# First block: context work two ticks earlier, its merge last in the tick, rounding as a one-element maximum, normalisation and epsilon on GpSimd

## What is computed

```python
# block 0
h = _ln(x, ln1_w, ln1_b) * (1 + sc1) + sh1
q, k, v = split(h @ Wqkv + bqkv)                 # 16 heads of 16
x = x + _attn(q, k, v) @ Wos + bos               # phase 0
h = _ln(x, ln2_w, ln2_b) * (1 + sc2) + sh2
x = x + _attn(h @ Wq + bq, context @ Wk + bk, context @ Wv + bv) @ Woc + boc   # phase 1
h = _ln(x, ln3_w, ln3_b) * (1 + sc3) + sh3
x = x + gelu(h @ W1 + b1) @ W2 + b2              # phase 2
# block 1: the same with 16 heads of 64, rotary q and k, a normalised context: phases 3, 4, 5
```

## Time and profile before

| | |
|---|---|
| median of 3 runs | 4402.54 us (4395.08 to 4405.3) |
| profiled execution | 4394.15 us, span of the core 4392.0 us |
| TensorE clock, mean | 0.987 |
| busy in the span | PE 94%, DVE 67%, ACT 63%, POOL 63% |
| POOL, one instruction | L1180 1.05 us, L1185 and L1190 1.3, L1209 1.02, L1220 0.75 |
| DVE, one instruction | L995 1.21 us, L1091 0.41, L1051 0.39, L1007 0.17, L1023 0.27 (two per batch) |
| DMAs of CX, issue to landing | 4.2 us (384 KB) and 3.8 us (128 KB) |
| DMA of X from the scratch | 4.0 us |

### The profile page before, as it was taken

One profiled execution on the slowest core, in us unless ns is written; L12 is line 12 of the kernel. 1 busy time (PEld: TensorE's weight loads), 2 busy tenths in 40 slices (PEclk: granted clock), 3 DMA queues, 4 the chain that ended last, 5 costly groups with the idle time before them and its releaser, 6 DMA issues.

```text
span 4392.0 us, 95934 instructions
## 1 busy us (share of the span) xinstructions
PE 4145.6 (94%) x34934; PEld 3514.9 (80%) x34934; DVE 2959.7 (67%) x6250; ACT 2745.7 (63%) x10788; POOL 2758.7 (63%) x2555
## 2 busy tenths in 40 slices
PE   7999989888889999999999999999999999999999
PEld 5777777777779987888888888778787878787998
DVE  7999988889865556555556565666666666665443
ACT  5999888888863335656565666656565656564332
POOL 4666666666667775555555565666666666665776
PEclk9999999999999999999999999999999999999999
DMA  2110011111111122222222222322222222221110
GB/s 74 33 33 30 31 41 37 45 45 36 44 55 49 40 73 80 73 75 73 73 75 73 73 78 86 101 75 85 74 86 74 86 73 86 74 91 61 49 46 33
DMA packets 229269, 276.65 MB, mean 63 GB/s; under 512 B 37948, under 2 KB 160320, under 8 KB 228800
## 3 DMA queue, kind: packets, MB, share of 16 engines
q1 hardware_dynamic: 228732, 270.51, 18.0%
q10 hardware_dynamic: 68, 0.02, 0.0%
HBM read 85.89 MB, written 50.33 MB: 31 GB/s over the span
## 4 chain that ended last, share of the span: by engine, by line
PE 65%; DVE 20%; ACT 8%; issue 5%; POOL 2%; DMA 0%; ACTq 0%; SPq 0%; POOLq 0%; DVEq 0%
PE BANKS L573 15%; PE BANKS L575 14%; PE BANKS L574 14%; PE BANKS L724 6%; PE BANKS L712 6%; PE BANKS L760 5%; DVE NM L995 4%; DVE PT L1002 3%; ACT PR L880 2%; ACT PR L864 2%; DVE WL L1044 1%; DVE Z L1101 1%; ACT HF L908 1%; DVE ST L1091 1%; PE BANKS L769 1%
## 5 line engine op out<-in xcount | busy, mean ns | idle before, releaser
L1180 POOL TENSOR_TENSOR PR<-PR,RL 128x512 f32<-128x512 f32 x1024 | 1069.5, 1045 | 946.0 <-DVE RL L1007 942.5
L880 ACT ACTIVATE PR<-BANKS,NM 128x128 f32<-128x128 f32 x2048 | 730.0, 384 | 487.8 <-DVE NM L1058 431.0
L864 ACT ACTIVATE PR<-BANKS,NM 128x128 f32<-128x128 f32 x2048 | 728.9, 415 | 3.9 <-DVE NM L995 3.8
L573 PE MATMUL BANKS<-HH,WH 128*128 128x512 f32 x1632 | 691.7, 424 | 38.0 <-DVE SN L1072 26.7
L1058 DVE TENSOR_REDUCE NM<-BANKS 128x8 f32<-128x1024 f32 x256 | 312.7, 1222 | 532.2 <-PE BANKS L724 532.1
L760 PE MATMUL BANKS<-ID,PR 128*128 128x128 f32 x4096 | 632.9, 278 | 40.6 <-DVE OL L1051 22.8
L575 PE MATMUL BANKS<-HH,WL 128*128 128x512 f32 x1632 | 644.5, 395 | 0.0
L574 PE MATMUL BANKS<-HL,WH 128*128 128x512 f32 x1632 | 644.2, 395 | 0.0
L760 PEld LDWEIGHTS BANKS<-ID,PR 128*128 128x128 f32 x4096 | 496.0, 142 | 165.1 <-issue 61.9
L864 ACT ACTIVATION_READ_ACCUMULATOR PR<-BANKS,NM 128x1 f32 x2048 | 520.1, 257 | 0.0
L1203 POOL TENSOR_TENSOR GL<-GF,GH 128x512 fp32r<-128x512 f32 x256 | 342.4, 1338 | 206.1 <-DVE GH L1147 206.1
(11 more groups left out here) (123 smaller groups left out, 10825.9 us busy)
## 6 DMA issues: line engine op xcount, KB each, us to landing
SW<-SN SPq DMA_DIRECT2D x1024, 128.0 KB, 2.0
x_scratch<-X SPq DMA_DIRECT2D x80, 512.0 KB, 3.2
X<-x_scratch SPq DMA_DIRECT2D x80, 512.0 KB, 4.0
CX<-in_ctx SPq DMA_DIRECT2D x32, 384.0 KB, 4.2
X<-in_x SPq DMA_DIRECT2D x16, 512.0 KB, 3.8
out<-X SPq DMA_DIRECT2D x16, 512.0 KB, 2.9
CX<-in_ctx SPq DMA_DIRECT2D x32, 128.0 KB, 3.8
STG<-in_L_xcond_W SPq DMA_DIRECT2D x4, 512.0 KB, 5.0
```

Source lines behind the costliest of these rows:

```text
L573: e.matmul(o, lh, rh, start=first and i == 0, stop=False)
L864: made = e.activation(pr[:, r], bank[:, r], ACT.Exp, bias=nm[:, h:h + 1], accum_out=RL[npr(t)[0]][:, h:h + 1])
L880: made = e.activation(pr[:, r], bank[:, r], ACT.Exp, bias=nm[:, h:h + 1], accum_out=RL[npr(t)[0]][:, h:h + 1])
L1180: e.tensor_tensor(p3, p3, RL[npr(t)[0]][:, :].unsqueeze(2).broadcast_to([128, 4, 128]), ALU.mult).then_inc(s_nrm, 1)
```

## The change

Four things, all in phases 0 and 1 (`p < 2`):

- `load_c`, `c_turn`, `c_hf` and `c_split` of phase 1 are two ticks earlier; `c_merge` keeps its tick, tg-10.
- On DVE `c_merge` moves from before `v_out` to behind `c_split`, for phase 4 too.
- The casts L1110, L1140 and L1012 become `tensor_reduce` with a maximum over an axis of one element; its output is fp32r as before.
- Epsilon (L1115) and the four normalisations per group (L1101) are done by GpSimd; there `norm` stands behind `root` and ahead of `bias`.

```diff
             if p in CROSS:
-                at["load_c", tg - (22 if p == 1 else 16)].append((p, g))
+                at["load_c", tg - (24 if p == 1 else 16)].append((p, g))
...
-                    at["c_turn", tg - (14 if p == 1 else 8) + c].append(Part(p, g, c, 0))
-                    at["c_hf", tg - (13 if p == 1 else 8) + c].append(Part(p, g, c, 0))
-                    at["c_split", tg - (12 if p == 1 else 7) + c].append(Part(p, g, c, 0))
+                    at["c_turn", tg - (16 if p == 1 else 8) + c].append(Part(p, g, c, 0))
+                    at["c_hf", tg - (15 if p == 1 else 8) + c].append(Part(p, g, c, 0))
+                    at["c_split", tg - (14 if p == 1 else 7) + c].append(Part(p, g, c, 0))
                 at["c_merge", tg - (10 if p == 1 else 5)].append((p, g))
...
+            def rounded(o, i, p):
+
+                if p < 2:
+                    return e.tensor_reduce(o, i.unsqueeze(2), AX, ALU.max)
+                return e.tensor_copy(o, i)
...
-                for p, g in at["c_merge", tick]:
-                    u, k = h_of(p, g, True)
-                    q.wait_ge(s_hl, 2 * u + 2)
-                    e.tensor_copy(HH[k][64:128, 1, :], HL[k][64:128, 1, :].bitcast(F)).then_inc(s_hm, 1)
-
                 for x in at["v_out", tick]:
...
                 for x in at["norm", tick]:
+                    if x.p < 2:
+                        continue
...
-                    e.tensor_copy(HH[k][:, x.c, :], HF[u % 2][:, x.c, :]).then_inc(s_hh, 1)
+                    rounded(HH[k][:, x.c, :], HF[u % 2][:, x.c, :], x.p).then_inc(s_hh, 1)
 
                 for p, g in at["root", tick]:
+                    if p < 2:
+                        continue
...
-                    e.tensor_copy(HH[k][:, x.c, :], HF[u % 2][:, x.c, :]).then_inc(s_hh, 1)
+                    rounded(HH[k][:, x.c, :], HF[u % 2][:, x.c, :], x.p).then_inc(s_hh, 1)
+
+                for p, g in at["c_merge", tick]:
+                    u, k = h_of(p, g, True)
+                    q.wait_ge(s_hl, 2 * u + 2)
+                    rounded(HH[k][64:128, 1, :], HL[k][64:128, 1, :].bitcast(F), p).then_inc(s_hm, 1)
...
                 for p, g in at["root", tick]:
                     u = xq(p, g)
                     q.wait_ge(s_half, 1)
+                    if p < 2:
+                        q.wait_ge(s_mv, 4 * u + 4)
+                        e.tensor_scalar(VE[u % 2][:, :], MV[u % 2][:, :, 1], 1e-5, None, ALU.add, ALU.bypass).then_inc(s_ve, 1)
                     q.wait_ge(s_ve, u + 1)
                     e.tensor_tensor(RS[u % 2][:, :], VE[u % 2][:, :], MH[:, :], ALU.pow).then_inc(s_rs, 1)
+
+                for x in at["norm", tick]:
+                    if x.p > 1:
+                        continue
+                    u = xq(x.p, x.g)
+                    q.wait_ge(s_rs, u + 1)
...
+                    made = e.tensor_scalar(Z[:, x.b, :], X[u % NX][:, x.b, :], MV[u % 2][:, x.b, 0:1], RS[u % 2][:, x.b:x.b + 1],
+                                           ALU.subtract, ALU.mult)
```

More of the change, by code:

```diff
@@ L1207, in _ @@
                     q.wait_ge(s_half, 1)
+                    if p < 2:
+                        q.wait_ge(s_mv, 4 * u + 4)
+                        e.tensor_scalar(VE[u % 2][:, :], MV[u % 2][:, :, 1], 1e-5, None, ALU.add, ALU.bypass).then_inc(s_ve, 1)
                     q.wait_ge(s_ve, u + 1)
                     e.tensor_tensor(RS[u % 2][:, :], VE[u % 2][:, :], MH[:, :], ALU.pow).then_inc(s_rs, 1)
+                for x in at["norm", tick]:
[3 more added lines that the diff above has]
+                    q.wait_ge(s_rs, u + 1)
+                    if u:
+                        pp, gg = divmod(u - 1, NG)
+                        q.wait_ge(s_turn, hparts["turn", Part(pp, gg, 1, 1 if KIND[pp] == "a" else 0)] + 1)
+                    made = e.tensor_scalar(Z[:, x.b, :], X[u % NX][:, x.b, :], MV[u % 2][:, x.b, 0:1], RS[u % 2][:, x.b:x.b + 1],
+                                           ALU.subtract, ALU.mult)
+                    if x.b == G - 1:
+                        made.then_inc(s_z, 1)
                 for p, g in at["c_root", tick]:
```

## The result

| | before | after |
|---|---|---|
| median | 4400.02 us | 4337.08 us (4 runs, 4334.57 to 4338.11) |
| ratio | 1 | 0.9856 [0.9839, 0.9873] |
| span of the profiled execution | 4392.0 us | 4332.8 us |
| TensorE clock, mean | 0.987 | 0.993 |
| period of a group, phase 0 / phase 1 | 35.94 / 39.95 us | 34.88 / 36.60 us |

The changed kernel is 1.4% faster: 63 us of the medians and 59 of the spans, where I had worked out 106. The direction and most of the mechanism held; the size didn't.

A forecast was written before the change was run, and what follows sets the result against it. Three nearly full engines in one ring, VectorE last, were taken to bound phases 0 and 1; gains of 26 us in phase 0 and 80 in phase 1, together 106, gave 4300 us, range 4262 to 4352.

The forecast's parts named there:

- The wait for V: Phase 1, tick -10: TensorE waits 2.7 us per group for the value's eviction behind the merge; forecast to go.
- the case that the wait only moves: Phase 1: bank order or later merge moves the 2.7 us elsewhere; 4360 us, chance 0.08.
- GpSimd's normalisation: Four tensor_scalar of 128x256 per group, taken at 0.55 us each, bounds 0.26 to 0.75; with epsilon +2.4 us.
- The burst at ticks -14 to -10: Phase 1: GpSimd's queue of 4.3 us in tick -14 and 2.9 in -13 delays its product; 0.2 us per group.
- The prologue: Kernel start: four normalisations in a row become 2.2 us on GpSimd beside the modulation; zero, within 1 us.
- the wait for OL: Phase 0: 1.0 us per group for VectorE's OL, within 1.9 us of waits forecast to shrink to 0.3.
- The new pair in tick -15: Phase 1's PSUM bank ring: two new waits without slack; bank changes put at 0.3 us, bounds 0 to 1.0.
- rival C: Phases 0 and 1: the maximum over one element is slow, up to 3.5 us; about 4507 us, chance 0.05.
- The merge's place: Last in its tick: removes the 0.70 us wait; phase 1 cost bounded 0 to 0.7 us, phase 4 zero.
- Rival A: Phases 0 and 1: ScalarE or GpSimd takes VectorE's place, 1.5 us per group; 4348 us, chance 0.17.
- signs of being wrong: Reductions over 1 us, GpSimd's tensor_scalar over 0.8, product waits over 1 per group, OL wait in tick -15, changed last stretch.
- signs of being right: L668's phase 1 wait under 0.7 us, clock 0.99, reductions 0.6 to 0.7, periods 34.3 and 35.0, VectorE under 85%.

The follow-up runs named there:

- N: The kernel before with only the normalisation and epsilon of phases 0 and 1 moved to GpSimd: 4406.5 us, ratio 1.0007.
- C: The kernel before with only the context two ticks ahead and the merge last in its tick: 4444.0 us, ratio 1.0098.
- C R: The changed kernel with epsilon and all normalisations back on VectorE: 4405.7 us, ratio 1.0013.
- N R: The changed kernel with the context's ticks as before, two ticks later, merge still last: 4389.5 us, ratio 0.9970.
- R: The kernel before with only the rounding as a maximum over one element in phases 0 and 1: 4390.4 us, ratio 0.9980.
- the fastest: The changed kernel with the first two groups' normalisation on VectorE and the context four ticks ahead of the kernel before: 4316.3 us, ratio 0.9804.

## Why the prediction was right in direction and too large

**Right: the place and the cure in phase 1.** The wait for V disappeared, the clock went to 1.00, and phase 0's period fell. Of the 3.35 us that a group of phase 1 gained, TensorE's busy time gives 1.87 (490.3/14 to 464.1/14 us for the same instructions) and its waits only 1.48: 2.7 removed, and 1.2 of others come in on balance. Not all of the 1.87 need be the clock's: in phase 0 the busy time fell too, from 33.27 to 32.78 us per group, with the clock at 1.00 in both. That is nearly half of phase 0's gain of 1.06, it wasn't in my sum, and why it fell is open.

**Right, with a gap: what leads to the wait.** I wrote that 0.70 and 1.25 us ahead of v_out are gone "by construction", and put the case that the wait only moves at 0.08. The combinations show how near that was: in each of N, C and C R the wait is there again at 2.3 to 3.4 us, in N R at 2.9. Two chains meet at `k`: GpSimd's second difference, and VectorE's own program up to v_out and the merge. N frees VectorE and delays the difference; C brings the difference in time and leaves VectorE late. R, which shortens a bit of VectorE, does little alone. The gains don't add: in phase 1, N costs 0.9 us per group, C costs 3.2, and both with R save 3.35. I had costed each part against the kernel before, not against the kernel with the others missing.

**Wrong, the largest term: GpSimd's normalisation.** I took 0.55 us, the lower half of the bounds of 0.26 to 0.75; it takes 1.24, above both. The upper end was the addition of two full operands, and I took it that a form with one full operand can't be dearer. The run without the multiplication shows 0.94 for one step: the second step, with its operand, costs 0.30 us, and one step alone is above my upper end. At 0.94 us, 14 us of the missing 47 came back. GpSimd stands at 27.67 and 30.14 us per group, not 25.4 and 28.0. The Trainium skill ("GPSIMD Engine Reference", section "Engine selection") says that elementwise work on a tile is about twice as slow there as on VectorE with two inputs, and runs at roughly line rate with one. The runs don't agree for this form: with per-partition operands it takes 1.24 us against 0.75 for an addition of two full operands of the same size. The epsilon, at 0.233 against 0.2, was right.

**Wrong: what that did.** The burst at ticks -14 to -10 was in the prediction, at 0.2 us per group; it is 1.3 (19.4/15). The prologue was "zero, within 1 us"; it is 12.6, of which 5.3 come from 4.87 and 4.83 us of four normalisations in a row, on which TensorE stands for 3.16 and 3.98 us, and the rest from a low clock after that, which some kernels without these waits show as well. I named the instruction and the place and then took the modulation for a cover without reading which of the two ends last.

**Wrong: the wait for OL.** I had let 1.9 us of phase 0's waits shrink to 0.3 because VectorE would be less late. It is 1.33 (1.0 and 0.33 for WL), and the 1.0 stands in phase 0 of every kernel of this study, whatever VectorE carries (15.6 us in 16 times with C alone, 14.1 in 14 in the fastest). It isn't lateness carried over: VectorE stood idle for 1.75 us at 325.99. From 326.85 it runs WL (1.41 us), the maximum, the copy and OL back to back (the changed kernel, DVE and PE):

```profile
328.18 1.22 DVE L1001 TENSOR_REDUCE NM<-BANKS 128x8 f32<-128x1024 f32 x1
...
329.31 0.68 DVE L1008 COPY PT<-BANKS 128x512 f32<-128x512 f32 x1
...
329.99 0.39 DVE L1052 TENSOR_TENSOR OL<-BANKS,OH 128x256 fp32r<-128x256 f32 x1
...
330.50 0.42 PEld L760 LDWEIGHTS BANKS<-ID,PR 128*128 128x128 f32 x4 [1.18 <-POOL PR L1190]
330.53 0.63 PE L760 MATMUL BANKS<-ID,PR 128*128 128x128 f32 x4 [1.00 <-DVE OL L1052]
```

Between the maximum and OL nothing was taken away. GpSimd's product comes in the same moment here (the PEld line), so an earlier OL alone might not end the wait. The new pair in tick -15 cost 0.7, inside its bounds of 0 to 1.0.

**Right.** The maximum over one element takes 0.676 us (0.673 to 0.687 over 96), the 0.68 that I took, so rival C is out: the maximum is slower than a free cast and faster than one that meets GpSimd. The Trainium skill ("VectorE: DVE Perf Modes", the perf-mode tier table) gives a reduction one element per cycle and no more; my estimate from its clock, 0.53 us plus overhead, is in line with the 0.676. ScalarE's waits are 0.76 us per group in phase 0, as forecast, and 0.93 in phase 1, where I had left them at 1.1. The merge's place, the loads and the rest of the program (3133.7 to 3132.0 us) cost nothing. VectorE gave up 4.3 us in phase 0, not 5.1: neighbouring instructions overlap by 0.08 us (the copy at 329.31 ends at 329.99, the reciprocal behind it starts at 329.91), which for five instructions gone is half of the difference.

**The sum.** Of 106 us, 12.6 were lost in the prologue, 8 in phase 0 (26 against 18.1) and 28 in phase 1 (80 against 52); 1.7 came back after it. Rival A, GpSimd as the next late engine, described phase 1 better than my forecast did: the run with one step, which changes nothing but GpSimd's instruction, gets back 0.73 us per group. Three of my signs of being wrong are there: tensor_scalar over 0.8 us on GpSimd (1.24), waits for its product over 1 us per group (1.3) and a wait for OL in tick -15 (0.7). With them stand the signs of being right: no wait of L668 in phase 1, the clock at 1.00, reductions without spread. The time fell inside the range, 37 us above the forecast.

Left open: why the clock in the prologue is low in some executions, and whether OL ahead of the maximum in VectorE's tick would end the wait of 1.0 us in phase 0 (that wasn't tried); and why TensorE's busy time in phase 0 fell at the same clock.

## What to carry to other kernels

When work moves from a late engine to an idle one, list what the receiving engine owes in those very ticks, and who waits for it: here the move gave nothing alone, since a difference was queued behind the moved work, and 50 us once that difference went ahead two ticks. Another two brought 8 us more, in part by other waits. Cost the parts of a change against each other's absence as well, since two chains that meet in one wait give nothing singly. And treat the pipeline's start as a stretch of its own: what is hidden in the steady state isn't there.

## What the hardware showed that I had not expected

- GpSimd's tensor_scalar on 128x256 with two per-partition operands and two steps takes 1.24 us and with one of each 0.94, longer than its addition of two full tiles, 0.75 us.
- A tensor_reduce over an axis of one element rounds 128x512 in 0.676 us with hardly a spread beside a busy GpSimd, where a cast takes 0.41 us free and 1.17 beside GpSimd's instructions. The Trainium skill ("SBUF — State Buffer", section "Who interferes with whom") says that copy, cast and tensor_scalar in their fast forms can contend with GpSimd, and tensor_reduce never does. All runs here agree: in the run with C alone, casts and normalisations went up to 1.26 and 1.25 us, while no rounding reduction in any kernel passed 0.69.
- TensorE's clock in phase 1 followed the long waits: 1.00 in the kernels without one of 2 us, 0.96 with R alone, 0.95 with C R and before, 0.94 with N R, 0.93 with N, 0.91 with C.
